# One fused transformer kernel: its opening stage rebuilt around pairs of projection tiles kept in PSUM, and the first row of maxima made by a product

## The reference, cut to what matters

```
latents = layernorm(x);  xn = layernorm(ctx, g, b)            # ctx: 77 rows of 192
ln      = layernorm(latents, ln_l_g, ln_l_b)
q       = ln @ Wq.T
k, v    = split(concat([xn @ Wkv.T, ln @ Wlkv.T]))            # 77 + 1024 keys
qn      = rmsnorm(q, qn_g) / 8;  kn = rmsnorm(k, kn_g)        # per head of 64
attn    = softmax(qn @ kn.T + mask of the context keys)
x       = x + (attn @ v) @ Wo.T + bo
```

## Time and profile before

| | us |
|---|---|
| median of three runs (872.8 to 876.67) | 875.1 |
| profiled execution, span from the first to the last instruction | 875.3 |
| TensorE busy | 782.6 (89%) |
| VectorE busy | 548.9 (63%) |
| ScalarE busy | 396.1 (45%) |
| GpSimd busy | 307.2 (35%) |
| first score product of head 0 starts | 61.40 |
| first score product of head 1 starts | 103.39 |

### The profile page before, as it was taken

The page is one execution under the profiler, slowest core; times in us unless marked ns, Lnnn a source line. Parts: engine busy times, 40 slices in busy tenths (PEclk is TensorE's granted clock), DMA queues, the critical chain, the costliest instruction groups (busy, mean ns, idle before and its releaser), DMA issues.

```text
span 875.3 us, 13078 instructions
## 1 busy us (share of the span) xinstructions
PE 782.6 (89%) x4960; PEld 634.2 (72%) x4960; DVE 548.9 (63%) x1219; ACT 396.1 (45%) x721; POOL 307.2 (35%) x289
## 2 busy tenths in 40 slices
PE   3779988999999999989989989887489999999996
PEld 3666554656665555577968979886379999999996
DVE  6677786667587585255543469894846556565552
ACT  3434543454445434455271244443117655566561
POOL 5413001200120013036362123433425576676773
PEclk9999999999999999999999999997699999999999
DMA  7000000000000010010003020112212354343522
GB/s 180 1 1 1 0 1 2 1 0 1 1 1 1 1 51 1 0 49 3 1 1 92 1 97 1 49 50 96 75 48 73 86 145 133 82 135 88 145 32 31
DMA packets 20111, 38.41 MB, mean 44 GB/s; under 512 B 4507, under 2 KB 15633, under 8 KB 17745
## 3 DMA queue, kind: packets, MB, share of 16 engines
q1 hardware_dynamic: 13393, 29.14, 10.1%
q0 software_dynamic: 6656, 8.43, 5.5%
HBM read 29.02 MB, written 8.40 MB: 43 GB/s over the span
## 4 chain that ended last, share of the span: by engine, by line
PE 58%; DVE 15%; ACT 4%; issue 4%; POOL 2%; DMA 0%; DVEq 0%; ACTq 0%; POOLq 0%
PE ps L453 18%; PE ps L1086 11%; PE ps L593 8%; PE ps L693 6%; PE ps L610 2%; PE ps L611 2%; PE ps L555 2%; DVE sm L1459 1%; ACT htmp L1958 1%; DVE rep L1647 1%; DVE Pb L1463 1%; PE ps L1026 1%; PE ps L1014 1%; DVE mxp L1254 1%; DVE sm L1468 1%
## 5 line engine op out<-in xcount | busy, mean ns | idle before, releaser
L593 PE MATMUL ps<-PT,VA 128*65 128x512 f32 (+1 forms) x288 | 147.2, 593 | 0.3 <-ACT PT L1900 0.2
L1900 ACT ACTIVATE PT<-ps 128x512 f32<-128x512 f32 x128 | 76.0, 595 | 62.2 <-PE ps L611 61.7
L1086 PE MATMUL ps<-he,wh 128*128 128x258 f32 x768 | 104.0, 288 | 0.0
L453 PE MATMUL ps<-GT,wh 128*128 128x258 f32 x768 | 99.0, 286 | 2.4 <-ACT het L2176 1.9
L453 PEld LDWEIGHTS ps<-GT,wh 128*128 128x128 f32 x768 | 94.0, 189 | 4.5 <-ACT het L2176 4.0
L1086 PEld LDWEIGHTS ps<-he,wh 128*128 128x128 f32 x768 | 95.4, 189 | 0.4
L1766 DVE TENSOR_TENSOR he<-het,he 128x516 fp32r<-128x516 f32 x64 | 44.6, 696 | 48.2 <-ACT he L1794 37.5
L2486 POOL DMA_INDIRECT out_dram<-ye,idx x40 | 66.9, 1672 | 22.5 <-DVE ye L1748 12.0
L2228 POOL TENSOR_TENSOR rs<-rs,half 128x4 f32<-128x4 f32 (+2 forms) x19 | 17.8, 938 | 156.7 <-DVE rs L1126 127.6
L2237 POOL TENSOR_TENSOR ssq<-ssq,half 128x4 f32<-128x4 f32 x32 | 32.3, 1008 | 115.6 <-DVE ssq L1198 115.4
L610 PE MATMUL ps<-QA,KA 128*128 128x512 f32 x144 | 68.3, 474 | 1.6 <-DMA QB<-mrt 1.6
(11 more groups left out here) (267 smaller groups left out, 1583.3 us busy)
## 6 DMA issues: line engine op xcount, KB each, us to landing
wr<-in_w1e_dram SPq DMA_DIRECT2D x8, 1024.0 KB, 4.9
wr<-in_w2e_dram SPq DMA_DIRECT2D x8, 1024.0 KB
x<-in_x_dram SPq DMA_DIRECT2D x4, 512.0 KB, 6.9
w<-in_w_dram SPq DMA_DIRECT2D x2, 1024.0 KB, 4.7
y_dram<-yr SPq DMA_DIRECT2D x3, 512.0 KB, 3.0
out_dram<-x SPq DMA_DIRECT2D x3, 512.0 KB, 4.4
gt<-y_dram,idx POOLq DMA_INDIRECT x40
out_dram<-ye,idx POOLq DMA_INDIRECT x40
```

Source lines behind the costliest of these rows:

```text
L453: op = pe.matmul(o, l, r, start=n == 0, stop=n == len(calls) - 1)
L593: pe.matmul(bank[6 + hf][0:65, :], VA[b][0:K, kt, h, :], PT[u % 4][0:K, :], start=kt == 0, stop=kt == 8).then_inc(p_pv, 1)
L1086: op = pe.matmul(bank[dc][:, 0:258], w2h[i][:, wc_], he[j][:, m, 258 * c:258 * c + 258], start=n == 0, stop=n == 23)
L1900: a.activation(PT[u % 4][0:K, :], bank[4 + u % 2][0:K, :], ACT.Exp, bias=0.0 if K == 128 else mcol[:, b:b + 1]).then_inc(a_exp, 1)
```

## The change

Only the first layer is changed, mostly its opening:

- **Loads.** Both halves of batch 0's x come first, then ctx, the small gains, and the 256 columns of wqk of heads 0 and 1; the constants and wc, wv, the other 256 columns and wo follow. The staging tiles lie in PT and beside OT instead of in qkn.
- **DVE order.** The moments of both halves of x come before both are centred; the two halves use four banks and four tiles tsp, so that ACT needs no wait for DVE between them. The context rows take gain and bias on ACT after their transpose (`lxg`, `lxb`) in place of two DVE products with rows (L1172, L1174).
- **Projections.** The q/k products of two tiles share one bank of 512 columns, and four such banks (2 to 5) stay filled: `project`, then `squares` on ACT for 512 columns at once, and `from_bank` on DVE, which multiplies straight from PSUM two tiles at a time. POOL takes eight powers at once. The v products of batch 0 move behind it: one pair before the first tile of maxima and one behind each of the first three. In the later `proj` pairs of tiles are used too, with sq doubled.
- **Heads.** The high part KB is copied from KA in SBUF and no longer from PSUM, and the low part of K waits for KA alone (`a_ka`). The masked context keys take the gain on ACT (`high_ctx`). The bank with the first K half is held until the context keys are masked (`v_kx`), because the mask reads its first column there, where before it was held until a column was copied (`v_kc`). kcn is written doubled by DVE, without the copy on POOL.
- **First row of maxima.** For the first four tiles of head 0 four small products of a column of maxima, repeated 65 times, with the identity put the row on partition 64 of PSUM, and ACT copies it negated into QB: no transpose, no DMA.
- **What moves on.** Of head 1's five steps three come before the first score product, the other two go beside head 0 (`second`), whose SIDE_RATE becomes 1.2 and whose MAX_AT starts at unit 6. Identity transposes of 84 become 80, at other places.

```diff
-MAX_AT = (4, 6, 7, 9, 10, 12, 13, 15)
-
-SIDE_RATE = (1.0, 1.4, 1.4, 1.0, 1.0, 1.0, 1.0, 1.0)
+MAX_AT = (6, 7, 9, 10, 12, 13, 15, 16)
+
+SIDE_RATE = (1.2, 1.4, 1.4, 1.0, 1.0, 1.0, 1.0, 1.0)
...
-                        busy[m] = (v_qb, 2 * H + gi + 1) if is_q else (v_kc, H + 1) if gi == 0 else (v_ka, 2 * H + 2)
+                        busy[m] = (v_qb, 2 * H + gi + 1) if is_q else (v_kx, H + 1) if gi == 0 else (v_ka, 2 * H + 2)
...
+                if qt == 4:
+                    pe.wait_ge(v_qb, 2 * hi + 2)
...
+            def turn_head(h, gi, j, m):
+                for t in range(4):
+                    op = pe.transpose(bank[m][:, 128 * t:128 * t + 128],
+                                      qkn[:, 4 * gi + t, j, :, :].rearrange("p a d -> p (a d)"), ident[:, :])
+                op.then_inc(p_ht, 1)
+
+            def first_row():
+                clear(0)
+                pe.wait_ge(v_mr, 1)
+                for t in range(4):
+                    op = pe.matmul(bank[0][0:65, 128 * t:128 * t + 128], mx[:, 0, t:t + 1].to_broadcast([128, 65]), ident[:, :],
+                                   start=True, stop=True)
+                op.then_inc(p_mT, 1)
+                busy[0] = (a_mrt, 1)
+
             two = lambda n: n % 2
...
+            warm(7, 40)
+            for g in range(2):
+                pe.wait_ge(v_z, g + 1)
+                drain(transposed(yb[g], g, lambda k: (0, 1, 6, 7)[2 * g + k], lambda k: (a_tsp, 2 * g + k + 1)))
+            warm(5, 16)
+            for j in range(4):
+                project(0, 0, j, 2 + j)
+                if j == 2:
+                    ctx_turned(0, 0)
+            ctx_product(0, 0, 1)
+            warm(6, 12)
+            pe.wait_ge(v_qkn, 1)
+            clear(6)
+            turn_head(0, 0, 0, 6)
+            busy[6] = (v_qb, 1)
+            clear(7)
+            turn_head(0, 0, 2, 7)
+            warm(1, 12)
+            pe.wait_ge(v_qkn, 2)
+            turn_head(0, 1, 2, 3)
+            turn_head(0, 1, 0, 4)
+            busy[3], busy[4] = (v_ka, 2), (v_qb, 2)
+            pe.wait_ge(v_kcn, 1)
+            pe.transpose(bank[5][:, 0:SC], kcn[:, 0, :, :].rearrange("p a d -> p (a d)"), ident[0:SC, 0:SC]).then_inc(p_kc, 1)
+            busy[5] = busy[7] = (v_kx, 1)
+            values(0, 0, 6)
+            second = head(0, 1, side)
+            for qt in range(4):
                 max_tile(0, qt)
-                next(h_, None)
-            max_row(0, 0)
-            drain(h_)
-            warm(3, 8)
-
-
-            beside = [spaced(proj(0, 1, side, False), head(0, 2, side)), spaced(head(0, 3, side), ln(1, side), ctx(1, side)),
+                if qt < 3:
+                    values(0, qt + 1, 7 - qt % 2)
+                if qt > 1:
+                    next(second)
+            first_row()
+            next(second)
+
+
+            beside = [spaced(second, proj(0, 1, side, False), head(0, 2, side)), spaced(head(0, 3, side), ln(1, side), ctx(1, side)),
                       spaced(proj(1, 0, side, True), head(1, 0, side)), spaced(head(1, 1, side)),
                       spaced(proj(1, 1, side, False), head(1, 2, side)), spaced(head(1, 3, side)),
...
+            def squares(q, src):
+
+                v.wait_ge(a_sq, q + 1)
+                c = slice(8 * (q % 4), 8 * (q % 4) + 8)
+                step(v.tensor_reduce(ssq[:, 0, c], src.rearrange("p (h d) -> p h d", h=8), AX.X, ALU.add))
+                settle()
+                v.tensor_scalar(ssq[:, 1, c], ssq[:, 0, c], 1.0 / DH, 1e-16, ALU.mult, ALU.max).then_inc(v_ms, 1)
+
...
+
+            def low_q(H, gi, m):
+                h, c = H % H0, slice(512 * gi, 512 * gi + 512)
+                v.wait_ge(a_qa, 2 * H + gi + 1)
+                v.tensor_tensor(QB[0:64, h, c], bank[m][0:64, :], f(QA[0:64, h, c]), ALU.subtract).then_inc(v_qb, 1)
+
+            def low_k(H, gi, m):
+                h, c = H % H0, slice(512 * gi, 512 * gi + 512)
+                v.wait_ge(a_ka, 2 * H + gi + 1)
+                return v.scalar_tensor_tensor(KA[64:128, h, c], bank[m][64:128, :], gg[64:128, 2:3], f(KA[64:128, h, c]),
+                                              ALU.mult, ALU.subtract)
+
+            def ctx_kept(H, m, first):
+
+                v.wait_ge(p_kc, H + 1)
+                step(v.tensor_copy(kc[:, 0:SC], bank[m][:, 0:SC]))
+                settle()
+                v.copy_predicated(kc[:, 0:80], mrow[:, H // H0, :], bank[first][:, 0:1].to_broadcast([128, 80])).then_inc(v_kx, 1)
...
+            drain(moments_x(0), moments_x(1), centred_x(0), centred_x(1))
+            halves_x(0, 0, tsp[0])
+            halves_x(0, 1, tsp[1])
+            drain(ctx_norm(0))
+            halves_x(1, 0, tsp2[0])
+            halves_x(1, 1, tsp2[1])
+            ctx_centred(0)
+            v.wait_ge(d_gg, 128)
             v.scalar_tensor_tensor(gg[:, 2:3], gg[:, 0:1], DH ** -0.5, gg[:, 1:2], ALU.mult, ALU.mult)
             step(v.tensor_copy(mcol[:, :], mcol8[:, :]))
...
+            def kept(q):
+                return qkr[:, 2 * (q % 2):2 * (q % 2) + 2, :].rearrange("p t n -> p (t n)")
+
+            def from_bank(q):
+                v.wait_ge(g_rq, q + 1)
+                return normalised(2 * q, 2, bank[2 + q])
+
+            squares(0, kept(0))
+            squares(1, kept(1))
+            squares(2, kept(2))
+            from_bank(0)
+            squares(3, kept(3))
+            from_bank(1).then_inc(v_qkn, 1)
+            ctx_squares(0)
+            from_bank(2)
+            low_q(0, 0, 6)
+            from_bank(3).then_inc(v_qkn, 1)
+            ctx_keys(0, 0)
+            low_k(0, 0, 7).then_inc(v_ka, 1)
+            ctx_kept(0, 5, 7)
+            low_k(0, 1, 3)
+            low_ctx(0).then_inc(v_ka, 1)
+            second = head(0, 1, side)
             for qt in range(4):
                 max_tile(0, qt)
-                next(h_, None)
-            drain(h_)
-
-
-            made["unit"] = 0
-            made["ctx_bank"] = 3
...
+            def high_k(H, gi, m):
+                a.wait_ge(p_ht, 4 * H + 2 * gi + 2)
+                copy(KA[:, H % H0, 512 * gi:512 * gi + 512], bank[m], gg[:, 2:3]).then_inc(a_ka, 1)
+
+            def again_k(H, gi):
+
+                h, c = H % H0, slice(512 * gi, 512 * gi + 512)
+                a.wait_ge(a_ka, 2 * H + gi + 1)
+                copy(KB[0:64, h, c], f(KA[0:64, h, c])).then_inc(a_kb, 1)
...
+            def halved(dst, src, landed):
+                a.wait_ge(*landed)
+                copy(dst, src).then_inc(a_whi, 1)
+
+            def squares(q):
+                a.wait_ge(p_qk, q + 1)
+                if q >= 2:
+                    a.wait_ge(v_ms, q - 1)
+                a.activation(qkr[:, 2 * (q % 2):2 * (q % 2) + 2, :].rearrange("p t n -> p (t n)"), bank[2 + q],
+                             ACT.Square).then_inc(a_sq, 1)
+
+            halved(wqk[0][:, :, 0:256], wqk_in[0], (d_wqk, 16))
+            a.wait_ge(d_ln, 64)
+            affine(0, 0, 0, tsp[0])
+            affine(0, 1, 1, tsp[1])
+            affine(1, 0, 6, tsp2[0])
+            affine(1, 1, 7, tsp2[1])
+            for q in range(3):
+                squares(q)
+            ctx_turned(0, 0)
+            squares(3)
+            halved(wv[0], wv_in, (d_wv, 32))
+            ctx_squares(0, 0)
+            ctx_values(0, 1)
+            halved(wqk[0][:, :, 256:512], wqk_in[1], (d_wv, 32))
+            high_q(0, 0, 6)
+            a.wait_ge(v_init, 1)
+            a.wait_ge(p_ht, 2)
+            high_k(0, 0, 7)
+            again_k(0, 0)
+            a.wait_ge(p_ht, 3)
+            copy(KA[:, 0, 512:1024], bank[3], gg[:, 2:3]).then_inc(a_ka, 1)
+            a.wait_ge(p_ht, 4)
+            copy(QA[:, 0, 512:1024], bank[4]).then_inc(a_qa, 1)
+            high_ctx(0)
+            again_k(0, 1)
+            values(0, 0, 6)
             a.wait_ge(g_wo, 1)
-            a.wait_ge(d_w, 160)
-            copy(wo[0], wo_in).then_inc(a_whi, 1)
-            beside = [spaced(proj(0, 1, side, False), head(0, 2, side)), spaced(head(0, 3, side), ln(1, side), ctx(1, 3)),
+            halved(wo[0], wo_in, (d_rows, 64))
+            second = head(0, 1, side)
+            for j in (1, 2):
+                values(0, j, 8 - j)
+            next(second)
+            values(0, 3, 7)
+            a.wait_ge(p_mT, 1)
+            copy(QB[64:65, 0, 0:512], bank[0][64:65, :], -1.0).then_inc(a_mrt, 1)
+            next(second)
+            next(second)
+
+
+            beside = [spaced(second, proj(0, 1, side, False), head(0, 2, side)), spaced(head(0, 3, side), ln(1, side), ctx(1, 3)),
...
+            def low(dst, src, high, n):
+                g_.wait_ge(a_whi, n)
+                g_.tensor_tensor(dst, src, f(high), ALU.subtract).then_inc(g_wlo, 1)
...
-                root_q(0, 4 + t)
-
-            g_.wait_ge(a_whi, 3)
-            g_.tensor_tensor(wo[1], wo_in, f(wo[0]), ALU.subtract).then_inc(g_wlo, 1)
+            low(wv[1], wv_in, wv[0], 2)
+            low(wqk[1][:, :, 256:512], wqk_in[1], wqk[0][:, :, 256:512], 3)
```

(6 more changed lines are left out.)

570 lines of the change are left out of this document (256 added, 314 removed).

## The result

The changed kernel takes 855.8 us (median of four runs, 853.8 to 857.6) against 875.9 us of the kernel before on the same chip (872.8 to 877.5): a ratio of 0.977, 95% interval 0.974 to 0.980. The forecast was 858.9 us, its range 852 to 867. The profiled execution has a span of 854.5 us and took 856.3 us with what lies around it.

A forecast was written before the change was run, and what follows sets the result against it. VectorE's chain was taken to bound the opening up to 61.4 us, TensorE the heads. 875.3 - 19.5 (opening) + 3.1 (head 0) + 2.0 - 2.0 (heads 1 to 7) = 858.9 us, range 852 to 867.

The forecast's parts named there:

- The load of the second half of x in time: Opening: second half of x, needed at 6.7 us, second in SP's queue; no wait taken, bound 2.5 us later.
- VectorE done with xt and the constants at 17.9: Opening: statistics, centrings, four roundings with low parts, context and constants on VectorE end at 17.9 us.
- Squares at 0.87 us each: Opening, from 17.9 us: four reductions of two tiles' squares, 0.7 us plus 0.17 scaling each, 3.5 in all.
- TensorE "isn't the bound there": Opening: four projections of two tiles, 1.43 us each, end at 20.5 us and don't hold up VectorE.
- Low parts of wv and wqk on POOL beside `from_bank`: Opening, 25 to 29 us: POOL's subtractions don't stop VectorE; nothing taken, bound 2.4 us.
- First tile of maxima at 31.2: Opening: K of head 0 complete at 30.8 us, first tile of maxima starts at 31.2 instead of 48.83.
- The maxima and the row: End of opening: tiles of maxima until 39.8 us, row by products and ACT copy until 41.0, first score product at 41.9.
- Head 0, +3.1: Head 0 longer by 3.1 us: 0.8 moved transposes, 1.0 waits at its start, 1.3 rows of head 1.
- Heads 1 to 7, +2.0 and -2.0: Heads 1 to 7: held K bank costs 0.35 us in each of six heads, 2.0; shorter waits for VectorE return 2.0.
- (a): Heads give more back: every mask costs 1.7 us and both rows 1.8; total 869.4 us, chance 0.14.
- (d): Ends slower: held K bank, mask a whole unit later, six heads pay 24.0 us; total 880.9 us, chance 0.02.
- rival (c): Heads gain: half of 12.7 us of gaps goes and rows in head 0 cost nothing; 851.3 us, chance 0.11.
- Rival (b): Opening disturbed: x late by 2.5 us and VectorE stopped by POOL for 2.4; total 863.8 us, chance 0.11.

The follow-up runs named there:

- steady_clock: Changed kernel with 50 idle transposes for 40 at the start, eight new between the transposed halves, ten for sixteen ahead of the projections: 863.1 us, ratio 0.971.
- the run by DMA: Changed kernel with the first row of maxima of head 0 sent as before, by transpose, ACT and DMA: 857.5 us, ratio 0.974.

## Why the prediction was right

Its time was 3.1 us above the median. Up to the last score product, the part that the change touches, it was 1.0 us above; the rest of the difference lies in code left alone. The mechanism is in the main the one it described, but one step failed, and in the opening two errors cancelled. By its steps:

- **The load of the second half of x in time: right.** It was there at 6.77, without a wait. Late, it would have cost 1.3 us where the trace was made so, and 2.5 was the bound.
- **VectorE done with xt and the constants at 17.9: 0.7 short.** It was 18.6. The missed terms are the centring beside the low part of wqk (0.8) and a rounding beside a fill on POOL (0.5); the rest of the row was 0.6 shorter than summed. "Ends about when the roundings begin" was right for the roundings and overlooked the centrings ahead of them. Moving the low part only moved the stop.
- **Squares at 0.87 us each, TensorE "isn't the bound there": wrong.** They came 1.43 apart, the pace of a pair of projections, because the first projection stood at 16.66 and not near 14. The step that failed is the start of the projections: I had the data ready at 14 and didn't ask at what clock the sixteen idle transposes ahead of them would run. In `steady_clock` they start at 14.53, and VectorE waits 0.2 us in all; in the changed kernel its gaps are 1.46 us where I had 0.3.
- **Low parts of wv and wqk on POOL beside `from_bank`: nothing, right.** In the changed kernel they run from 27.43 to 29.94, and the VectorE operations beside them have their usual 0.68, 1.21, 0.67 us. The Trainium skill, page "SBUF — State Buffer", section "SBUF: two separate sides", lets these pass, since they have at most one input in SBUF, and the trace agrees; it also agrees for the subtraction of two SBUF tiles that took 2.17 us in the run with the v products inside.
- **First tile of maxima at 31.2: 32.35.** The sum of the above. At full clock it comes at 30.42 to 30.81 in four runs, earlier than forecast, and that is partly luck: in the run by DMA, where VectorE doesn't wait for squares, the work from the constants to the tile took 12.1 us where the forecast had 13.3, and that made up for the 0.7 that VectorE was late.
- **The maxima and the row: right in the sum.** 8.3 us from the first tile to the end of the reduction for 8.6, then 2.0 to the score product for 2.1. Within the 2.1 the make was another: the four products took 1.06 us (eight records), not 0.6, and the last wait, 0.45, is for ACT's copy of the row and not for VectorE's low parts of Q. The forecast of 41.9 met 42.59 here and 40.65 to 43.87 over all executions with the row, the v products and the banks as in the changed kernel. That TensorE's clock would fall behind a wait for the DMA I hadn't seen.
- **Head 0, +3.1: +2.7, of another make.** At a clock of 1.00 it takes 43.4 us in six other traces, +1.4, and that is TensorE's own work (40.18 for 38.69): the eight transposes, 1.3 us by their rows of 0.60 and 0.66 and not 0.8. In sum its waits are no longer than before, 3.2 us of gaps for 3.3. Of the 1.0 for the start 0.8 was there, the wait for the mask; but the waits for rows and maxima, which I had longer by 1.3, got shorter. The kernel before had 1.8 and the 1.1 below, the changed kernel 0.5 and 0.2:

```profile
PE ps L555 <- ACT mrt L1794: 1.1, 1, 1.1
```

```profile
PE ps L560 <- DVE kc L1305: 0.8, 1, 0.8
...
PE ps L595 <- DVE mx L1340: 0.5, 2, 0.3
...
PE ps L585 <- ACT mrt L1885: 0.2, 1, 0.2
```

In the trace of the changed kernel the other 1.2 us are a clock of 0.96. It fell at 67.13, behind a wait of 0.89 us: twelve projections took 2.93 us there, and 1.69 behind the same wait in the second trace of this kernel.
- **Heads 1 to 7, +2.0 and -2.0: 1.2 shorter.** The held bank cost 1.6, near the 2.0, and in these heads it fell in two waits of 2.2 us together, not in six (a third, 0.8, is in head 0). The relief was then 2.8. Rivals (a) and (d) are ruled out by the waits: 2.9 us for the mask in all. The longest is 1.5, though, where I had each below 1: that sign failed.
- **The remaining 3.5 us** are the difference of the spans behind the last score product, in code left alone. The kernel before differs by 5.4 us from itself there, 4.6 of them in the expert layer. What makes that layer vary I can't say: it went by chip in eleven of the traces, with no wait of TensorE at 191.8 us and with 5.0 us of waits for ACT's het in the one of 201.8.

So rival (c), with gains in the heads, is part of it: the rows cost less than before. Rival (b) also is: VectorE was stopped for 1.3 us, at another place than I had looked.

Of the 18.8 us of the opening four parts were taken back one by one: the place of the v products (6.45), the four banks (5.7, with a fall of the clock in it), the order of the loads (1.3) and the row (0.7). The rest, VectorE's new order, the pairs and the steps of head 1 that moved, is argued from the timeline and wasn't taken back singly.

## What to carry to other kernels

Keeping products in PSUM so that the engines ahead can run on was worth more than the copies it saves, where SBUF had room for only half of them. Products put back among the projections made TensorE set the pace and cost nearly their whole length. When an opening is short of work, ask at what clock its fill-in transposes will run: give the start of the next real product for both levels, and compare two traces only after checking that this start is the same. When a POOL operation is moved, look at everything on VectorE that it may meet at either end, not only at the operation that it met before.

## What the runs showed of the hardware

- **The clock behind a pause.** After 1.62 to 2.31 us of pause behind the first idle transposes the eight real ones still ran at full speed (1.09 us), but the next eight, after another 1.18, took 1.61 to 1.97 (four traces). With pauses of 0.72 to 1.21 ahead of the first they took 1.09 again (four traces). But so did they after 2.05 in the run with x late, which I can't explain. What sorts all nine traces is how long the forty idle transposes ahead had taken: 5.89 to 6.52 us where the clock fell, 7.01 to 7.49 where it didn't. Pauses of at most 0.35 us had no slow transposes behind them, in two runs. The granted clock read 1.00 or 0.50 there, 2.4 and 1.2 GHz, and mixes.
- **Its price differs by what comes next.** The same fall cost 1.6 us ahead of the projections (16.66 for 15.08) and 1.8 us in the first units of head 0 (46.48 for 44.68). In head 0 of the changed kernel, behind a wait of 0.89 us, it cost 1.2.
- **POOL stops VectorE also in small things.** A fill of one row of 768 elements (0.73 us) took a rounding from 0.42 to 0.89, and a subtraction of 1.28 us took one centring from 0.41 to 1.23. It goes the other way too: beside a product of 1.22 us out of SBUF a power of POOL took 2.54 instead of 1.64 us (the run with the copies in SBUF), and nothing of the kind is seen beside the product out of PSUM.
